# A selective scan with four engines: who spreads the rows of C, and through which PSUM bank

## What is computed

```python
def step(h, xs_t):                       # along the 2304 pixels of direction k
    d_t, u_t, B_t, C_t = xs_t
    dA = jnp.exp(d_t[..., None] * A)
    h = h * dA + (d_t * u_t)[..., None] * B_t[:, :, None, :]
    y = jnp.einsum('bkdn,bkn->bkd', h, C_t)      # n: 16 states
    return (h, y)
delta = jax.nn.softplus(dts + dt_b[None, :, :, None])
```

## Time and profile before

| | us |
|---|---|
| median of 3 runs (14314.65 to 14317.07) | 14314.98 |
| the profiled execution | 14321.17 |
| its span, first to last instruction | 14319.4 |
| scan stage of one image (of eight) | 1259.3 |

### The profile page before, as it was taken

One profiled execution on the slowest core, in us unless ns is written; L12 is line 12 of the kernel. 1 busy time (PEld: TensorE's weight loads), 2 busy tenths in 40 slices (PEclk: granted clock), 3 DMA queues, 4 the chain that ended last, 5 costly groups with the idle time before them and its releaser, 6 DMA issues.

```text
span 14319.4 us, 281562 instructions
## 1 busy us (share of the span) xinstructions
PE 12173.0 (85%) x71128; PEld 7344.9 (51%) x71128; DVE 12205.0 (85%) x13653; ACT 12188.8 (85%) x28586; POOL 9892.3 (69%) x4006
## 2 busy tenths in 40 slices
PE   6887988889888898888988889888898888988889
PEld 4554555545555455554555545555455554555545
DVE  8999779997799967999679986899858998599985
ACT  6998789987889878998889978899788997889978
POOL 5999069980699807998079970899708996099960
PEclk9999999999999999999999999999999999999999
DMA  3443024440344303443034430344303442044420
GB/s 117 134 134 125 28 95 132 134 127 22 101 132 133 121 22 106 133 142 105 22 115 132 143 98 22 120 133 143 91 22 128 132 142 85 22 134 132 142 79 27
DMA packets 908190, 1470.82 MB, mean 103 GB/s; under 512 B 38912, under 2 KB 891904, under 8 KB 893664
## 3 DMA queue, kind: packets, MB, share of 16 engines
q1 hardware_dynamic: 906560, 1452.37, 32.1%
HBM read 1350.07 MB, written 102.17 MB: 101 GB/s over the span
## 4 chain that ended last, share of the span: by engine, by line
PE 31%; issue 29%; ACT 15%; POOL 14%; DVE 9%; ACTq 1%; DVEq 0%; DMA 0%; POOLq 0%; SPq 0%
POOL area L1652 11%; PE ps L710 9%; DVE area L1110 6%; ACT ps L1430 5%; PE ps L946 4%; PE ps L927 4%; ACT area L1385 4%; PE ps L688 4%; PE ps L697 2%; POOL area L1662 2%; POOL area L1641 1%; PE ps L792 1%; DVE area L360 1%; ACT hst L1353 1%; PE ps L736 1%
## 5 line engine op out<-in xcount | busy, mean ns | idle before, releaser
L1110 DVE TENSOR_TENSOR_SCAN area<-ps,area 128x385 f32<-128x385 f32 x9216 | 8102.7, 940 | 312.1 <-ACT ps L1430 266.5
L1652 POOL TENSOR_TENSOR area<-area 128x1152 f32<-128x1152 f32 x3072 | 7995.3, 2638 | 45.7 <-POOL area L1641 45.7
L1430 ACT ACTIVATE ps<-area,a_neg 128x384 f32<-128x384 f32 x9216 | 5110.6, 579 | 334.9 <-DVE area L1110 311.8
L710 PE MATMUL ps<-area,ident 128*128 128x384 f32 x10368 | 3905.7, 509 | 332.1 <-POOL area L1662 207.6
L688 PE MATMUL ps<-ident,area 128*128 128x128 f32 x12096 | 2114.9, 284 | 1352.7 <-ACT area L1385 1348.5
L710 PEld LDWEIGHTS ps<-area,ident 128*128 128x128 f32 x10368 | 1909.7, 197 | 1814.1 <-ACT area L1409 401.7
L1385 ACT ACTIVATE area<-ps,area 128x384 f32<-128x384 f32 x4032 | 2310.2, 573 | 536.5 <-PE ps L688 536.1
L688 PEld LDWEIGHTS ps<-ident,area 128*128 128x128 f32 x12096 | 1388.8, 141 | 2614.3 <-ACT area L1385 2048.3
L1595 ACT ACTIVATE area<-ps,t_neg,area 128x384 f32<-128x384 f32 x3456 | 2127.7, 668 | 111.2 <-PE ps L927 23.6
L1636 POOL TENSOR_TENSOR area<-area,ones 128x2304 f32<-128x2304 f32 x8 | 43.6, 5446 | 3067.6 <-ACT area L1333 2947.9
L697 PE MATMUL ps<-ident,area 128*128 128x128 f32 x12096 | 2027.4, 277 | 131.0 <-ACT area L1385 129.9
(11 more groups left out here) (142 smaller groups left out, 10552.7 us busy)
## 6 DMA issues: line engine op xcount, KB each, us to landing
area<-bc_rows SPq DMA_DIRECT2D x1536, 768.0 KB, 6.7
xz<-x_normed SPq DMA_DIRECT2D x144, 288.0 KB, 3.6
area<-in_x SPq DMA_DIRECT2D x18, 1728.0 KB, 10.1
area<-x_padded SPq DMA_DIRECT2D x24, 1250.0 KB, 5.8
z_raw<-z_st SPq DMA_DIRECT2D x144, 192.0 KB, 2.8
area<-z_raw SPq DMA_DIRECT2D x8, 3456.0 KB, 12.6
x_padded<-x_st SPq DMA_DIRECT2D x120, 200.0 KB, 7.3
x_normed<-area SPq DMA_DIRECT2D x9, 1728.0 KB, 7.9
```

Source lines behind the costliest of these rows:

```text
L710: m = e.matmul(ps[:, 5 + j, 0:CH], ident[:], hb[i % NH][:, j], start=i == 0, stop=i == N - 1)
L1110: e.tensor_tensor_scan(track(HB, i, j, k), rev(ps[:, 2 + j, side(k):side(k) + WIDE], k), track(DBU, i, j, k), 0.0, ALU.mult, ALU.add).then ...
L1430: e.activation(ps[:, 2 + j, 1:1 + CH], dlt[:, par, j], ACT.Exp, scale=a_neg[:, j, k, i:i + 1]).then_inc(da, 1)
L1652: e.tensor_tensor(dbu[i % NH], du[:, par], row_b[:, q % 2, i % ROWS:i % ROWS + 1].broadcast_to([128, J, CH]), ALU.mult).then_inc(dbus, 1)
```

## The change

Three sets of states change hands: GpSimd keeps the products of two states (0 and 9), seven states are turned (14 in place of 13), and VectorE has seven (2, 4, 5, 8, 11, 13, 15) in place of six.

The C rows of VectorE's states are no longer copied by ScalarE. Sixteen rows of C of a chunk are loaded once (16 partitions x 384), and TensorE spreads row n by a matmul whose weight is column n of the identity, repeated 128 times, into bank 1. It waits for VectorE's product before and, for rows 4, 8 and 11, for a delta, since the softplus's logarithm also goes to VectorE through bank 1. Delta tiles (X0 to X2) and projections (U0, U1) join the turns in bank 0, in the order of the table `MAIL`. ScalarE reads the first item of a slot after exp (i, 1), and the second after `hold_state` and `head`, at the end of its iteration. The logarithms stand after exp (i, 0) of states 5, 8 and 11, the deltas after the scans of states 4, 7 and 10. Heads are written for two states at once. One of the three y stores moves to the end of iteration 3. The core of the diff:

```diff
-POOL_N = (0, 4, 9)
-TURN_N = (1, 3, 6, 7, 10, 12, 13)
-TURN_AT = {2: (0,), 3: (1, 2), 4: (3, 4), 5: (5,), 7: (6, 7), 8: (8, 9), 9: (10, 11), 11: (12, 13), 12: (14,),
-           13: (15, 16), 14: (17, 18), 15: (19, 20)}
+POOL_N = (0, 9)
+TURN_N = (1, 3, 6, 7, 10, 12, 14)
+X0, X1, X2, U0, U1 = ("x", 0), ("x", 1), ("x", 2), ("u", 0), ("u", 1)
+MAIL = {1: (X0,), 2: (0,), 3: (1, 2), 4: (3, X1), 5: (4, 5), 6: (X2,), 7: (6, 7), 8: (8, 9), 9: (10, 11), 10: (U0,),
+        11: (12, 13), 12: (14,), 13: (15, 16), 14: (17, U1), 15: (18, 19), 16: (20,)}
+ORDER = [item for m in MAIL for item in MAIL[m]]
-SUM_AT = {0: 3, 2: 4, 4: 6, 5: 7, 8: 10, 9: 12, 11: 13, 14: 16, 15: 17}
+SUM_AT = {0: 3, 2: 4, 4: 6, 5: 7, 8: 10, 9: 12, 11: 13, 13: 15, 15: 17}
-DELTA_AT = {1: 0, 4: 1, 7: 2}
-X_AT = {2: 0, 5: 1, 8: 2}
+ROW_AT = {2: 2, 5: 4, 6: 5, 9: 8, 12: 11, 14: 13, 16: 15}
-LN_AT = {i: j for i, op, j in SOFT if op == "ln"}
+STEP_AT = {4: 0, 7: 1, 10: 2}
+LN_AFTER = (2, 5, 8)
+ROW_AFTER = {4: 0, 8: 1, 11: 2}
...
+            def c_row(g, k, c, r):
+                e.wait_ge(hcp, g * NP + (r + 1))
...
+                e.dma_start(row_c[:, r], rows[k % 2:k % 2 + 1, n, ds(pos(k, c), CH)].broadcast_to([128, CH]))\
+                    .then_inc(c_in[r], 16)
+            def c_group(g, k, c, par, made):
+                e.wait_ge(c_ps, made)
...
+                e.dma_start(c_rows[:, par], rows[k % 2][n:n + N, ds(pos(k, c), CH)]).then_inc(c_rows_in[par], 16)
...
+                def bank_free(g, item, nxt, h):
+                    at = ORDER.index(item)
+                    done = [q for q in ORDER[:at] if isinstance(q, int)]
+                    if at and not isinstance(ORDER[at - 1], int):
+                        read(g, ORDER[at - 1], nxt, h)
+                    e.wait_ge(turn_cp, g * NT + (NT + (done[-1] + 1 if done else 0)))
...
+                def c_row(g, par, n, nxt):
+                    d = DVE_N.index(n)
+                    e.wait_ge(hcs, g * ND + (1 + d))
+                    if d == 0:
+                        e.wait_ge(c_rows_in[par], g * 8 + (16, 8)[par])
+                    if nxt and n in ROW_AFTER:
+                        e.wait_ge(dp_v, g * 3 + (3 + ROW_AFTER[n] + 1))
+                    e.matmul(ps[:, 1, 0:CH], ident[0:N, n:n + 1].broadcast_to([N, 128]), c_rows[:, par],
+                             start=True, stop=True).then_inc(c_ps, 1)
...
+                def slot(g, m, k, c, par, nxt, h):
                     for i in SUM_ORDER:
                         if SUM_AT[i] == m and i in POOL_N:
                             state_sum(g, i)
                     now, before = turns(m), turns(m - 1)
                     if now:
-                        turn(g, now[0])
-                    if before:
+                        post(g, now[0], k, c, nxt, h)
+                    if before and isinstance(before[-1], int):
                         turned_sum(g, before[-1])
+                    if m in ROW_AT:
+                        c_row(g, par, ROW_AT[m], nxt)
                     for i in SUM_ORDER:
                         if SUM_AT[i] == m and i in DVE_N:
                             state_sum(g, i)
                     if len(now) == 2:
-                        turn(g, now[1])
+                        post(g, now[1], k, c, nxt, h)
                         turned_sum(g, now[0])
...
-                    e.wait_ge(c_ps, g * ND + (ND + d + 1))
+                    e.wait_ge(c_ps, g * ND + (d + 1))
...
-                    slot = ar(DBU + i % NH * SLOT + side(k), J * WIDE).rearrange("p (j w) -> p j w", j=J)
-                    e.activation(slot[:, :, 0 if k < 2 else CH], hst[:, i], ACT.Copy).then_inc(heads, 1)
-                def c_copy(g, i, nxt, h=None):
...
-                    e.activation(ps[:, 1, 0:CH], row_c[:, q % 2, i % ROWS], ACT.Copy).then_inc(c_ps, 1)
+                    pair = ar(DBU + i % NH * SLOT, 2 * SLOT).rearrange("p (s w) -> p s w", s=2)
+                    pair = pair[:, :, side(k):side(k) + J * WIDE].rearrange("p s (j w) -> p s j w", j=J)
+                    e.activation(pair[:, :, :, 0 if k < 2 else CH], hst[:, i:i + 2], ACT.Copy).then_inc(heads, 1)
...
+                def collect(g, par, k, c, m, j, nxt, h):
                     now = turns(m)
-                    if len(now) == 1 and j == 1:
-                        turned_product(g, k, c, now[0])
-                    if len(now) == 2 and j != 1:
-                        turned_product(g, k, c, now[j // 2])
+                    item = now[0] if now and j == 1 else now[1] if len(now) == 2 and j == J else None
```

More of the change, by code:

```diff
@@ L505, in scan_rows @@
                 alone(e)
-                b_group(e.snap(b * 24), 0, 0, 0)
+                g0 = e.snap(b * 24)
+                b_group(g0, 0, 0, 0)
+                c_group(g0, 0, 0, 0, g0 * ND)
+                for r in range(NP):
+                    c_row(g0, 0, 0, r)
                 e.wait_ge(xp_dv, b * 12 + 8)
@@ L690, in turn, with post @@
                     i.then_inc(turn_mm, 1)
+                def post(g, item, k, c, nxt, h):
+                    if isinstance(item, int):
+                        turn(g, item, nxt, h)
+                    elif item[0] == "x" and nxt:
+                        bank_free(g, item, nxt, h)
+                        delta_tile(*nxt, item[1])
+                    elif item[0] == "u" and h is not None:
+                        bank_free(g, item, nxt, h)
+                        unit(k, h, item[1])
+                def c_row(g, par, n, nxt):
[7 more added lines that the diff above has]
+                             start=True, stop=True).then_inc(c_ps, 1)
                 def turned_sum(g, at):
@@ L711, in state_sum, with unit @@
                     m.then_inc(ysum, 1)
-                def slot(g, m):
+                def unit(k, h, i):
+                    e.wait_ge(xz_in, h * 16 + 16)
+                    for t in range(CT):
+                        at = i * DI + k * 128
+                        m = e.matmul(ps[:, 0, 0:CH], w_in[:, t, at:at + 128], xz[:, t], start=t == 0, stop=t == CT - 1)
+                    m.then_inc(unit_mm, 1)
+                def slot(g, m, k, c, par, nxt, h):
                     for i in SUM_ORDER:
@@ L754, in body @@
                             e.wait_ge(ct_cp, b * GM + GM)
-                        slot(g, m)
+                        if m < 2 and last:
+                            slot(g - 1, N + m, *last, 1 - par, (k, c), None)
+                        slot(g, m, k, c, par, nxt, h)
                         if m in ADD_AT:
@@ L765, in scan_phase @@
                 g = e.snap(b * 24 + 23)
-                slot(g, N)
-                slot(g, N + 1)
+                for m in (N, N + 1):
+                    slot(g, m, K - 1, NC - 1, 1, None, None)
             def back(b):
@@ L1299, in _, with softplus @@
             group_std(1, 0)
-            def softplus(g, par, k, op, j, bank=1, h=None):
+            def softplus(g, par, k, op, j, bank=0):
                 x, y = dlt[:, par, j], du[:, par, j]
@@ L1314, in softplus @@
                     e.wait_ge(dp_a, g * 9 + SOFT_N["exp", j])
[L1315 to L1320, removed]
+                    if bank == 0:
+                        e.wait_ge(hcs, g * ND + (2 + DVE_N.index(LN_AFTER[j]) - ND))
+                        bank = 1
                     e.activation(ps[:, bank, 0:CH], y, ACT.Ln, bias=1.0).then_inc(dp_a, 1)
@@ L1472, in scan_phase @@
                 g = e.snap(b * 24 + 23)
-                c_copy(g, N - 1, None)
-                for at in turns(N - 1):
+                for at in turns(N - 1) + turns(N):
                     turned_product(g, K - 1, NC - 1, at)
```

136 lines of the change are left out of this document (64 added, 72 removed).

## The result

The changed kernel takes 16,029.26 us, median of four runs (15,990.12 to 16,040.68), against 14,315.88 for the kernel before beside it (14,314.65 to 14,317.07): 1.119 times as long (95% interval 1.117 to 1.121). The prediction was 15,700, so slower as forecast, and 329 us slower than forecast. The profiled execution is the fastest of the four, 15,990.12 us with a span of 15,988.2.

A forecast was written before the change was run, and what follows sets the result against it. GpSimd and VectorE share the bound; a chunk goes from 52.5 to 52.0 (VectorE's work) + 7.3 (waits) + 0.6 (clock) = 59.9 us. 14,321 + 1,390 - 6 = 15,705, rounded to 15,700 us, range 14,780 to 16,200.

The forecast's parts named there:

- Mechanism and sign: VectorE's products wait for rows queued on TensorE behind turns that wait for ScalarE; slower, at 0.93.
- delta 0: VectorE's delta waiting for ScalarE's logarithm, late behind two y stores at state 5: 0.4 us even k, 0.6 odd.
- the row matmul: TensorE's seven rows a chunk, priced as the even-k addition: 0.64 us start to start, 0.81 to its end.
- the walk: Queue times counted through TensorE and ScalarE to each VectorE wait: 6.25 us a chunk even k, 8.3 odd, mean 7.3.
- The clock: TensorE's low granted clock doubles turn, turn-sum and row at row 15: 1.2 us in half the chunks, 0.6 a chunk.
- the 2 us off the first and the last chunk: An image's first chunk stores nothing, its last prepares nothing: some 2 us off each, 32 us in all.
- VectorE's own time: VectorE's work per chunk with the seventh product and short gaps: 50.5 + 1.24, then 52.0 us.
- The product's waits: VectorE's C product waits for TensorE's rows some 1,000 to 1,200 us in all, longest about 3 at state 11.
- Rival 1: Rows come in time, so VectorE's 52.0 us a chunk decides: 14,225 us; chance 0.06.
- Rival 2: Only row 11 waits, short waits vanish in quicker hand-offs: 55.0 us a chunk, 14,800 us; chance 0.12.
- Rival 3: Waits thin out TensorE's work, two more low-clock stretches a chunk add 460 us: 16,150 us; chance 0.09.
- Rival 4: TensorE's row costs something else: 14,800 us if nothing, 16,400 at the strided addition's price; chance 0.05.

## Why the prediction was right, and where its sizes were off

**Mechanism and sign: right.** The rows are late because of their place in TensorE's queue behind turns that wait for ScalarE, and the longest wait is at state 11. VectorE's idle time, us per chunk, averaged by place over the regular chunks (first and last of an image left out):

| ahead of | predicted, even / odd k | after, k = 0, 1, 2, 3 | rows over 128, k = 0, 1, 2, 3 |
|---|---|---|---|
| product 15 | 0.65 | 0.83 0.83 0.83 0.83 | 0.64 0.64 0.64 0.64 |
| delta 0 | 0.4 / 0.6 | 0.46 0.69 0.46 0.83 | 0.41 0.69 0.47 0.68 |
| product 4 | 1.0 | 1.24 1.24 1.24 1.24 | 1.05 1.05 1.05 1.05 |
| product 5 | 0 to 0.2 | 0 0.14 0 0.14 | 0 0.14 0 0.14 |
| product 8 | 0.75 / 1.4 | 0.91 1.56 0.91 1.56 | 0.72 1.37 0.72 1.37 |
| product 11 | 2.7 / 3.3 | 2.85 3.73 2.85 4.70 | 2.66 4.36 2.66 4.47 |
| product 13 | 0.65 | 0.83 0.83 0.83 0.83 | 0.64 0.64 0.64 0.64 |
| scan (2, 2) | none | 0.91 0.03 0.72 0.36 | none |
| whole chunk | 58.3 / 60.3, and 0.6 of clock | 60.05 61.39 59.89 62.98 | 57.98 61.24 58.11 61.32 |

**The step that was mis-sized: the row matmul**, "0.64 start to start, 0.81 to its end", taken from the addition "since columns and layout are the same". The layout was not: 16 partitions, not 128. The last column is the kernel for which that price held (0.65 and 0.81), and the walk comes out within 0.1 at nearly every place; row 11 of the odd chunks waits 3.3 us too where the granted clock was 1.00, and 4.4 where it was not. Its time is 15,722 us; that this is so near the forecast is partly luck, since the clock that was counted on row 15 fell on row 11. In the chunks of k = 0 the price is 58.93 us with 64 partitions (the same row times as 16, and steady at 58.9 from chunk to chunk) less 57.98 with 128. The odd chunks pay the same at each row, at a clock of 1.00 also at row 11 (3.5 with 16 or 64 partitions, 3.3 with 128): 0.95 x 192 = 182 us of the 329. The prediction bounded the price from 0 to 1.27 and gave "sixteen of 128 rows could be cheap" as the lower end; the shape difference turned out to cost, not save.

The Trainium skill (TensorE: Matmul & The Clock Gate, "Why this matters for your kernels") was weighed there: a single matmul over 32 rows takes the time of one over 128. The instructions alone come near that (0.48 to 0.58 against 0.49), but between neighbours over 128 the row costs 0.34 more, which that table does not count; the measurement decides.

**The clock: right in kind, wrong in place and size.** Predicted were 0.6 us a chunk on row 15. Row 15's wait is 0.83 throughout; the low level struck elsewhere: ahead of scan (2, 2), which waits 1.3 to 1.5 us in 60 of the 176 regular chunks (an even chunk then takes 60.6 us, not 58.9), and at row 11 in all regular chunks of k = 3 and 11 of the 48 of k = 1. One of the longest of those waits, with the granted clock of the stretch in the last line (0.50, the 1.2 GHz level):

```profile
7299.29 0.90 PE L730 MATMUL ps<-ident,area 128*128 128x128 f32 x3 [2.73 <-ACT area L1425]
7299.98 0.85 PE L761 MATMUL ps<-ident,area 128*128 128x128 f32 x3
7300.62 1.49 PE L820 MATMUL ps<-area,ident 128*128 128x384 f32 x2
7301.93 3.77 PE L774 MATMUL ps<-area,ident 128*128 128x384 f32 x6
...
7307.32 1.35 DVE L1190 TENSOR_TENSOR area<-area,ps 128x1152 f32<-128x1152 f32 x1 [5.79 <-ACT hst L1408]
...
7298.50:7305.30 6.80, 6.01 (x14) 3.86 (x15) 3.02 (x4) 2.90 (x7) 6.56 (x4) 0.50 0.23 62
```

TensorE had waited 2.73 us for ScalarE, without a projection to do in k = 3; state 9's sum then took 3.77 us against 2.10. Chunks with a granted clock of 1.00 throughout took 58.93 us for even k and 61.24 for k = 1, 60.1 in the mean; all regular chunks took 61.0. So the clock cost some 0.95 us a chunk, not 0.6.

**The miss, added up.** The profiled execution took 15,988 us, 279 more than 14,319 + 1,390. The scan stages took 11,706, which is 242 more than forecast: about 150 in the chunks at full clock (60.1 for 59.3: the row's price, less 0.17 a chunk by which the walk was too long), 67 by the clock, and 32 for the 2 us off the first and the last chunk, which did not come (60.3 and 60.1 us). Outside the scan stages, which the forecast left as they were, it is 4,282 for 4,245, 37 more; no run tells why. The other 50 are no mechanism: the median lies 39 us above the profiled execution where it was put 6 below, and 5 were rounded off.

**Smaller points.** VectorE's own time, predicted 52.0: a chunk less its waits is 52.0 (k = 0). The hop from a row's end to VectorE is 0.126, not 0.05. The product's waits, predicted 1,000 to 1,200 us, are 1,500: five rows with 0.2 more, and the clock. GpSimd's 49 us a chunk is as said, ScalarE's 45.9 and TensorE's 48.8 to 51 are 2 to 3 above.

**Rivals.** Rival 1 is refuted: row 11 comes 2.85 us late or more. Rival 2: the short waits do not vanish, they are longer than forecast. Rival 3 (16,150) is partly true: the low clock cost more than counted, though less than that. Rival 4's ends were wrong: the row cost more than an addition, less than a strided one.

**What stays open.** With the rows made cheap and early and state 4 back on GpSimd 273 us remain over the kernel before. There ScalarE waits 1,154 us for turns, and TensorE is busy 87% of the span: bank 0's chain is the likely holder, but no run took the delta tiles out of it alone.

## What to carry to other kernels

Work given to the engine with slack costs nothing only if its result is not wanted soon; with a deadline, walk the in-order queue ahead of it to the latest predecessor, and count the hand-overs between the engines. Moving such work forward pays less than the wait it removes, since what it passes becomes late instead. Price a matmul by a row of the same partition count, among neighbours of the same count, as well as the same columns: here padding the operand to the neighbours' 128 partitions was the cheapest gain of all.

## What was not expected of the hardware

A matmul over 16 or 64 partitions between others over 128 cost TensorE's queue 0.34 us more than one over 128. Its own two instructions took 0.48 to 0.58 us, against 0.49. But its first weight load, and that of the matmul behind it, were not run ahead: the one began 0.20 us after the start of the turn-sum's last matmul, where with 128 partitions it began within 0.01, and the other 0.41 us after the start of the row's second. The Trainium skill (TensorE: Matmul & The Clock Gate, "The mechanism") says that a weight load overlaps a running matmul only if they use different row groups, and just before that the background weight buffer also allows it. Here loads over the same rows overlapped (128 behind 128, 16 behind 16), and so did 128 behind 96; those that changed from 128 to 16 or 64 or back waited. What tells 96 from 64 no run shows.

The same program order with 64 partitions in place of 16 ran at a mean granted clock of 0.985 instead of 0.972, in equal row times, and also where no row stands, outside the scan stages (0.974 and 0.961); what sets this off no run tells.
